# Eight weight slots for adapter 1, the query and key weights turned ahead of the row product, ids by ScalarE's queue, scores in bank 0

## The reference

```python
x = adapter(itok_B_1_2, x, L0_...)                 # layer 0
x = mlp_block(x, itok_B_17_1546, L1_...)           # layer 1
x = adapter(itok_B_1_2, x, L2_...)                 # layer 2
x = adapter(itok_B_1_2, x, L3_...)                 # layer 3
# adapter: y = x + gelu(x @ W_down[role] + b_down[role]) @ W_up[role] + b_up[role]
#          layernorm(y) * gamma[role] + beta[role]        (W_down 256x128, W_up 128x256)
# mlp_block: att = softmax((x Wq)(x Wk)^T / 16) (x Wv) Wp + bp
#          cms = gelu(att cW1 + cb1) cW2 + cb2 + one_hot(code)
#          clip(x + cms + gelu([att, cms] mW1 + mb1) mW2 + mb2, 0, 1)
```

## Time and profile before

| What | Value |
|---|---|
| Runs, median | 221.39 us |
| The profiled execution's own time | 221.08 us |
| Its span (first to last instruction) | 219.3 us |
| PE busy | 185.2 us (84% of the span) |
| DVE busy | 122.0 us (56%) |
| ACT busy | 82.7 us (38%) |
| POOL busy | 71.5 us (33%) |
| Mean granted clock of TensorE | 0.987 |
| Share of the chain that ended last: PE, DVE, issue, ACT, DMA, SP's queue | 68, 13, 6, 4, 3, 3% |

### The profile page before, as it was taken

How to read it: one execution, slowest core, us unless ns; L and a number is a source line. 1 busy time by engine, 2 the same in 40 slices (tenths; PEclk the granted TensorE clock), 3 DMA queues, 4 the chain that set the end, 5 groups by cost and what they waited for, 6 DMA issues and landing times.

```text
span 219.3 us, 3238 instructions
## 1 busy us (share of the span) xinstructions
PE 185.2 (84%) x1101; PEld 160.0 (73%) x1101; DVE 122.0 (56%) x304; ACT 82.7 (38%) x174; POOL 71.5 (33%) x82
## 2 busy tenths in 40 slices
PE   0599967779986899999999999999998799897620
PEld 0588856769864688878888888899997798896410
DVE  5967672794598724996492520225455366536450
ACT  1352733443345903673244440055522344310400
POOL 8386281006245044563360400000133123114232
PEclk9999999999999999999999999999999999999995
DMA  3787389000996011040000000001034321040001
GB/s 98 232 246 202 105 244 245 33 0 4 276 278 199 17 32 64 0 161 34 0 0 0 3 0 0 0 0 51 6 93 145 95 67 54 25 144 24 24 3 48
DMA packets 18298, 17.84 MB, mean 81 GB/s; under 512 B 1953, under 2 KB 16618, under 8 KB 18282
## 3 DMA queue, kind: packets, MB, share of 16 engines
q1 hardware_dynamic: 17096, 14.98, 22.4%
q0 software_dynamic: 1120, 2.63, 4.3%
q10 hardware_dynamic: 66, 0.02, 0.0%
HBM read 16.58 MB, written 1.05 MB: 80 GB/s over the span
## 4 chain that ended last, share of the span: by engine, by line
PE 68%; DVE 13%; issue 6%; ACT 4%; DMA 3%; SPq 3%; POOL 1%; DVEq 0%; ACTq 0%; POOLq 0%
PE bank L603 16%; PE bank L605 15%; PE bank L604 15%; PE bank L721 5%; PE bank L707 5%; DVE g_l L1317 4%; PE bank L700 3%; DMA wuA<-in_L_cond_W_up 2%; PE bank L766 2%; PE bank L665 1%; DMA role_col_i<-in_itok_B 1%; PE bank L653 1%; PE bank L731 1%; SPq L560 1%; ACT g_h L964 1%
## 5 line engine op out<-in xcount | busy, mean ns | idle before, releaser
L1317 DVE TENSOR_TENSOR g_l<-g_full,g_h 128x512 fp32r<-128x512 f32 (+1 forms) x40 | 36.6, 924 | 31.0 <-ACT g_h L964 30.8
L961 ACT ACTIVATE g_full<-bank,vecs 128x512 f32<-128x512 f32 (+1 forms) x40 | 24.2, 604 | 47.9 <-PE bank L605 37.2
L1432 POOL TENSOR_TENSOR rstdA<-rstdA,power 128x1 f32<-128x1 f32 x16 | 9.4, 590 | 50.6 <-DVE rstdA L1181 50.5
L964 ACT ACTIVATE g_h<-bank,vecs 128x512 fp32r<-128x512 f32 (+1 forms) x40 | 23.9, 598 | 0.0
L1396 POOL TENSOR_TENSOR mw_l<-stage,mw_h 128x1024 fp32r<-128x1024 f32 x6 | 15.3, 2546 | 22.2 <-DVE mw_h L1175 22.2
L603 PE MATMUL bank<-ao_h,mw_h 128*128 128x256 f32 (+1 forms) x48 | 16.7, 348 | 0.0
L1396 POOL TENSOR_TENSOR cw_l<-stage,cw_h 128x1024 fp32r<-128x1024 f32 x4 | 10.8, 2714 | 17.6 <-DVE cw_h L1175 17.6
L603 PE MATMUL bank<-ao_h,cw_h 128*128 128x512 f32 x32 | 13.2, 413 | 3.7 <-ACT g_h L964 3.7
L603 PE MATMUL bank<-g_h,mw_h 128*128 128x256 f32 (+1 forms) x48 | 16.2, 338 | 0.0
L603 PE MATMUL bank<-cms_h,mw_h 128*128 128x256 f32 (+1 forms) x48 | 15.3, 318 | 0.0
L604 PE MATMUL bank<-cms_l,mw_h 128*128 128x256 f32 (+1 forms) x48 | 15.3, 318 | 0.0
(11 more groups left out here) (232 smaller groups left out, 457.6 us busy)
## 6 DMA issues: line engine op xcount, KB each, us to landing
stage<-in_L_cond_mW SPq DMA_DIRECT2D x6, 512.0 KB, 3.5
wdA<-in_L_cond_W_down SPq DMA_DIRECT2D x20, 128.0 KB, 2.5
wuA<-in_L_cond_W_up SPq DMA_DIRECT2D x20, 128.0 KB, 2.9
stage<-in_L_cond_cW SPq DMA_DIRECT2D x4, 512.0 KB, 4.0
wdB<-in_L_cond_W_down SPq DMA_DIRECT2D x10, 128.0 KB, 2.3
wuB<-in_L_cond_W_up SPq DMA_DIRECT2D x10, 128.0 KB, 3.0
table_gamma<-in_L_cond_ln_w SPq DMA_DIRECT2D x1, 384.0 KB, 6.1
table_beta<-in_L_cond_ln_b SPq DMA_DIRECT2D x1, 384.0 KB, 8.1
```

Source lines behind the costliest of these rows:

```text
L961: act.activation(g_full[n % 2][:, 0:width], bank[b][:, 0:width], ACT.Gelu, bias=bias)
L964: act.activation(g[0][:, j, 0:width], bank[b][:, 0:width], ACT.Gelu, bias=bias).then_inc(g_high, 1)
L1317: dve.tensor_tensor(g[1][:, j, 0:width], g_full[n % 2][:, 0:width], g[0][:, j, 0:width].bitcast(F32), ALU.subtract).then_inc(g_ready, 1)
L1432: pool.tensor_tensor(var[:, k, 1:2], var[:, k, 0:1], power[:, :], ALU.pow).then_inc(done, 1)
```

## The change

- **Slots.** Passes 4 to 7 of layer 0 load into adapter B's four slots, which nobody else uses until layer 3. So layer 0 has eight slots. `home(layer, n)` gives adapter and place for each pass; TensorE and SyncE both ask it.
- **Piece 1** is issued after all ten passes of layer 0.
- **Front of TensorE.** The transposes of Wq and Wk come first, then the row product, the transpose of Wv, the first fold, and only then `chunk_vecs`, `vectors` and the first `load`. ScalarE's copy of the ids (`spread`) moves behind its copies of the transposes.
- **Queues.** The 32 role ids in a column (`role_col_i[:, 0:1]`), Wq and Wv are issued by ScalarE, ahead of its eleven small DMAs. SyncE issues the roles, Wk, Wp and then the code ids, on a semaphore of their own (`codes_in`).
- **VectorE.** Before the ids only `lower`, `past`, `past_third`, `seq_col` and `tok_col` are computed. `third_of`, `low_row`, `third_mask`, `role_row_of` and `row_role` move behind `chunk_role_i`, in front of `role_hot`, `role_pick` and `from_row_i`.
- **GpSimd.** The clearing of `bu_rows` moves behind the making of `ident`, with a semaphore step of its own, for which SyncE waits.
- **Banks.** The scores of half 0 go to bank 0.

```diff
-PROJECT_BANKS, SCORE_BANKS = (0, 4), (2, 7)
+PROJECT_BANKS, SCORE_BANKS = (0, 4), (0, 7)
...
+USERS = {"A": [(0, n) for n in (*range(WSLOTS), *range(2 * WSLOTS, PASSES))] + [(2, n) for n in range(PASSES)],
+         "B": [(0, n) for n in range(WSLOTS, 2 * WSLOTS)] + [(3, n) for n in range(PASSES)]}
+
+
+def home(layer, n):
+
+    kind = "A" if (layer, n) in USERS["A"] else "B"
+    return kind, USERS[kind].index((layer, n))
...
-    steps = [("order",), ("chunk_vecs",), ("fold_transpose", 0), ("fold_transpose", 1), ("vectors",), ("fold", 0, 0), ("load", 0, 0),
-             ("fold", 0, 1), ("fold_low", 0)]
+    steps = [("fold_transpose", 0), ("order",), ("fold_transpose", 1), ("spread",), ("fold", 0, 0), ("fold", 0, 1),
+             ("chunk_vecs",), ("vectors",), ("load", 0, 0), ("fold_low", 0)]
...
-            sp.dma_start(role_col_i[:, 0:1], a["itok_B_1_2"].rearrange("(b o) -> b o", o=1)).then_inc(ids_in, 16)
-            sp.dma_start(role_col_i[:, 1:2], a["itok_B_17_1546"].rearrange("(b o) -> b o", o=1)).then_inc(ids_in, 16)
-            for n, pair in enumerate((("L1_cond_Wq", "L1_cond_Wk"), ("L1_cond_Wv", "L1_cond_Wp"))):
-                for m, w in enumerate(pair):
-                    sp.dma_start(tiled(n)[:, KD * m:KD * (m + 1), :],
-                                 a[w].rearrange("(k p) n -> p k n", p=P)).then_inc(stage_in[n], 16)
+            for m, w in enumerate(("L1_cond_Wk", "L1_cond_Wp")):
+                sp.dma_start(tiled(m)[:, KD:2 * KD, :],
+                             a[w].rearrange("(k p) n -> p k n", p=P)).then_inc(stage_in[m], 16)
+            sp.dma_start(role_col_i[:, 1:2], a["itok_B_17_1546"].rearrange("(b o) -> b o", o=1)).then_inc(codes_in, 16)
...
+                kind, i = home(layer, n)
+                slot, down, up, done = (i % WSLOTS, *((wdA, wuA, wA_in) if kind == "A" else (wdB, wuB, wB_in)))
+                if i >= WSLOTS:
+                    user, m = USERS[kind][i - WSLOTS]
+                    if user == 3:
+                        sp.wait_ge(upB_ps, place_of(3, passes_of(3)[m][0]) + 1)
+                    else:
                         sp.wait_ge(upA_ps, lane_a(user, passes_of(user)[m][0]) + 1)
...
-                if n == 7:
-                    piece(1)
+            piece(1)
...
+            act.dma_start(role_col_i[:, 0:1], a["itok_B_1_2"].rearrange("(b o) -> b o", o=1)).then_inc(ids_in, 16)
+            for m, w in enumerate(("L1_cond_Wq", "L1_cond_Wv")):
+                act.dma_start(tiled(m)[:, 0:KD, :],
+                              a[w].rearrange("(k p) n -> p k n", p=P)).then_inc(stage_in[m], 16)
...
-            pool.memset(bu_rows[:, :, :], 0.0)
             pool.affine_select(out=ident[:, :], in_=ident[:, :], compare_op=ALU.not_equal, fill=1.0, base=0,
                                pattern=[[-1, P]], channel_multiplier=1).then_inc(constants, 1)
+            pool.memset(bu_rows[:, :, :], 0.0).then_inc(constants, 1)
```

## The result

The changed kernel takes 220.5 us (median of 20 runs, 219.25 to 221.7) against 221.86 us before (20 runs, 219.55 to 224.29). The ratio is 0.9944, 95% interval 0.992 to 0.9968: 0.7 to 1.8 us faster. The prediction of 218.2 us had the sign right and the time 2.3 us too low; its range, 217.2 to 219.8, doesn't hold the result. Executions that ran slow throughout at a lower granted clock (in every kernel some do) are left out of all ratios, and the two of them that were profiled (e2, w4) out of all counts. The profiled execution took 219.93 us, span 218.1 against 219.3.

The account below looks back on a forecast made before the run. It took TensorE to bound the MLP phases, leaving gains only in the first 50 us. Slots -2.3, front -0.75 and bank 0 gave 218.0 from 221.08 and 218.3 from 221.39; predicted 218.2 us, range 217.2 to 219.8.

Parts of the forecast that it names:

- the term of -2.3 us: Layer 0's last windows: eight slots end TensorE's wait for passes 8 and 9; projection at 32.75 instead of 35.08.
- theory E: Follow-up theory: SyncE's queue, not TensorE's slot release, sets the last weights; later, the low front clock sets first `down`.
- rival 2: Layer 0's weights: half the wait stays because SyncE's issue also stops for other reasons; 219.7 us, chance 0.07.
- the term of -0.75 us: Front: reordered queues and transposes start the first `down` 1.0 us earlier, of which 0.8 remains; bounds +0.3 and -1.2.
- both at about 0.73 with the same 2.85 land near 3.6: Front: role ids and roles, issued first on two queues, land 0.9 us before the former 4.50.
- land by 1.2 + 3.8 = 5.0: Front: Wk and Wq, issued near 1.2 us, land by 5.0, perhaps 0.4 later for sharing the engines.
- the 0.7 us forecast: VectorE's front: five instructions moved before `from_row_i` spend about 0.7 of the 0.9 us gained on the ids.
- if both weights came 2 us late and held the row product: Front term's slow bound: late Wk and Wq hold the row product, making the term +0.3 us.
- rival 1: Front brings nothing: low clock lasts through the fold, or late Wq and Wk hold the row product; 219.1 us, chance 0.17.
- The clock in the front: TensorE's front: a fold at 1.2 GHz would take 3.6 to 4.4 us, with `load` at 12.8 to 13.1.
- The scores' bank, 0: Half 0's attention: `values` starts 1.2 us earlier, but `mix` waits for softmax and VectorE; term 0, bounds 0 and -1.2.
- rival 4: Slower: TensorE's clock falls in the new gap before `mix`; 228 us, or 223 for half of it; chance 0.04.

Follow-up runs that it names:

- e2: Kernel before with eight slots for layer 0, piece 1 behind the weights and the scores of half 0 in bank 0; ratio 0.9972.
- w4: Changed kernel with 16 filler matmuls on TensorE from about 2.5 us until its first transposes; no ratio.
- f2: Changed kernel, but SyncE and ScalarE issue the four projection weights only when both id loads have landed; ratio 1.0064.
- f3: Changed kernel with the row product ahead of the transposes of Wk in TensorE's order; ratio 0.9955.
- w5: Eight slots, old front, and 11 filler matmuls on TensorE ahead of the row product; ratio 0.9925.
- after again: The changed kernel, unchanged, run and profiled a second time; 220.91 us, no interval.
- w3: Kernel before with eight slots, 18 fillers in front, the scores in bank 0 and six fillers ahead of the first mix; ratio 0.9951.
- g2: Kernel before with eight slots for adapter 1, piece 1 still between its weights; ratio 0.9938.
- first and fourth series: First: slots, bank or mix fillers varied, ratios 0.9934 to 0.9972. Fourth: fillers in TensorE's front, ratios 0.9925 to 1.0051, one without.
- e3: Changed kernel with the scores of half 0 back in bank 2; ratio 0.9934.

## Why the prediction was wrong, step by step

**The weight slots: the step that failed is the term of -2.3 us**, "2.10 us of waiting go". The mechanism was right. Every profile with eight slots has 1.72 to 1.75 us from the eighth `down` to the projection, and no wait. The last weights were issued at 24.98, as forecast. But I took the wait of one execution for the wait of the kernel. The second profile of the same kernel had 0.5 us of it, and the slots would have saved 0.3 us there (2.03 - 1.73), against 2.3 in the first (4.00 - 1.73). The front is not what differs, as I thought when I wrote the expectations on theory E: pass 7's weights keep their 7.64 us ahead of the eighth `down` whether it is early or late. It is SyncE's stall behind them, of 1.86 and 1.08 us, and the landing of the last load, 1.24 us apart. What sets these two stays open. Timed over many executions, eight slots with the old front give 0.9952 and 0.9938: -1.1 and -1.4 us, from 221.4. That is half of the term, and fits the 1.3 us that the six profiles with four slots have in the mean. My rival 2 (half the wait stays, because "SyncE's issue also stops for other reasons") saw the stall of 1.86 us, but as a thing that would remain. It was part of the wait in before, and with eight slots no profile waits.

**The front: the term of -0.75 us had the wrong sign** in the profiles, +0.2 to +0.3 at like clock: full clock at 13.3 and 13.5 went with first `down`s of 14.74 and 14.84 with the old front, at 13.3 and 13.65 with 15.05 and 15.13 with the new one. Timed alone it is 0.9986 (0.9951 to 1.002), between -1.1 and +0.4 us, so that the sign is the profiles' alone; a gain of 0.75 us is not excluded by the timing. The failed steps: "both at about 0.73 with the same 2.85 land near 3.6" (the roles took 3.8), and "land by 1.2 + 3.8 = 5.0" (Wk 6.7; "perhaps 0.4 later" was too little). With the weights issued beside the ids both took longer; holding the weights back (f2) brought the ids to 3.86. The price of the five moved instructions was near the 0.7 us forecast (from `chunk_role_i` to `from_row_i` 1.08 us in f3, 0.48 before), but with the ids no earlier it was a loss and not a part of a gain. And the price I had put at the edge of this term, "if both weights came 2 us late and held the row product", is what happened, as rival 1 had it. The order then made TensorE's wait for Wk a wait of the row product.

**The clock in the front** I weighed, as a fold of 3.6 to 4.4 us; f2's took 3.75. But I treated it as a thing that the change would alter, not as one that differs from one execution of the same kernel to the next, from 12.03 to 14.94. This moved the first `down` by 1.4 us and everything behind it as far, but for the wait for weights; the two profiles of before end at 219.3 and 218.8 because the wait differed by more, the other way. The Trainium skill ("TensorE: Matmul & The Clock Gate", Part 1) says just this, that the number of matmuls at the lower clock varies between runs of one kernel, and that the ramp costs under 1% of a typical span. The profiles agree: first `down` at 14.17 and 15.56, 0.6% of the span. By its Part 4 a transpose doesn't reach the full clock; w5's twelve in 1.53 us, 0.13 each, say otherwise.

**The scores' bank, 0: right.** From projection to mix it is 11.22 to 11.25 in every profile, with either bank. "TensorE idles in another place" came true with its price: **rival 4 happened in part**. In the four profiles with bank 0 and no filler ahead of the mix (after, after again, f2, f3), the clock fell in the first mix twice; it cost 0.2 us to the second projection and 0.3 behind it in one, 0.4 in the other. With bank 2 or with fillers it never fell there, in fourteen profiles. (The counts in the expectation of w3 took in e2's profile and, by mistake, g2, which has bank 2.) I had written that it "decides from 3.05 us on"; the fall lasted 3.4 us and cost 0.5 in one profile, 0.4 in the other. That fillers or bank 2 make the kernel faster isn't shown: 0.9934 and 0.9938 against 0.9944.

**Sum.** -1.1 to -1.4 for the slots (each measurement +-0.8), about 0 for the front, 0 to +0.5 for the bank make -0.6 to -1.4; measured -0.7 to -1.8, with 1.24 in the middle. The forecast gain was 3.2: of the 1.95 us too much about 1.1 is the slots', 0.75 the front's, the rest the clock's. The fall in layer 3, 1.1 us in three of eighteen profiles, stood in no term. Open is what holds ScalarE, VectorE and SyncE between the first and the fourth `down`, which takes 7.0 to 7.3 us in ten profiles and 7.9 to 11.6 in the eight of the first and fourth series, all from two of the chips; no run took it apart. No kernel here is shown to beat the changed one.

## What to carry to other kernels

A wait read in one profiled execution is a sample. If what precedes it differs between executions, as a stall of the issuing queue and the landing of a load did here, profile the same kernel more than once before pricing the wait. Before giving a reason for such a difference, find an event that stands at a fixed distance from the engine that waits (here pass 7's issue, 7.64 us ahead in six profiles): only what differs behind it can be the reason. A small load on which all depends came sooner with the queues to itself (3.86 instead of 4.59 us), but that is not worth having at the price of the work that would keep TensorE busy: f2 lost more from the late clock than it won.

## What the hardware did that I had not expected

- Ids and weights on two queues: the 16 KB of roles took 3.8 to 4.3 us instead of 2.9 in five of six profiles (2.8 in one, e3, where the column of ids took 3.9 instead of 2.9), the 256 KB of Wk 5.5 to 5.9 instead of 3.8 in the four that show it.
- One SyncE issue of 0.4 us stood for 0.8 to 1.9 us, somewhere between 23.9 and 29.3 us, beside a 16 KB load of instructions, in thirteen profiles.
- The granted clock fell after 2 us in which TensorE was busy for 0.44 us, and in another execution of the same kernel (0.69 us busy) it did not.
- Transposes of 128x128 f32 took 0.13 us each at full clock (w5) and 0.23 at the lower level (before).
- From the second projection to the end all eighteen profiles take 170.0 us, but for one fall in the mix (+0.3) and three in layer 3 (+1.1).
